# L1 attention: tiles of |q - k| moved from VectorE to ScalarE, and part of their sum moved into an adding DMA

## The chip, the cores and the metric

One core of one Trainium2 chip runs the whole program in one launch. The metric is the device time in microseconds (us). The kernel before takes 2713.21 us, the median of three runs (2711.84 to 2714.14).

## The reference, cut to what matters

The program is a small vision tower on 128 images of 64 tokens of 64 numbers: a wavelet tokeniser, attention, a mixture of experts, then the layer in question, and a routed MLP. The layer in question is an attention whose logits are L1 distances:

```python
v = (x @ wqv_w.T + wqv_b)            # 8 heads: q, vf, vb, 64 wide each
k = x[:, :, None, :] * wk[None, None]
a[b, s, t, h] = -sum_w |q[b, s, h, w] - k[b, t, h, w]| / 8     # w: 64 numbers
a = softmax over s of (a with one row of zeros added)
o = (a with vf + a^T with vb), summed over the heads
y = o * sigmoid(1.702 * o);  h = x + x_normed + y @ fanin_w.T + fanin_b
```

For one image the scores are 64 x 64 x 8 = 32768 sums over 64 numbers each; there are 128 images, 64 pairs of two.

## The kernel before, in words

Each engine has its own program, written by hand; semaphores (the dictionary `X`) order them. The layer runs over 64 pairs `q`, and over the two images `b` of a pair. `s = 2q + b` counts images.

**TensorE** writes, for one image, 16 tiles of q - k. A tile is 128 partitions x 1024 float32 (16 sums of 64 numbers in each partition), two banks of PSUM, written by two matmuls of 512 columns against `pick`, a matrix of 1 and -1, with the fp16 halves of q and k in `blocks` as the moving operand. `ORDER = "DADDADDADDADDADD"` says who takes each tile: D is VectorE (11 tiles, banks 0 to 3, two tiles in turn), A is ScalarE (5 tiles, banks 4 and 5 together). Between tiles, at fixed positions `k` of this order, TensorE does the rest of the layer (`extra`): values, queries and keys of pair q + 1 in float32 (`values_b`, `values_f`, `queries`, `low`, `keys`), the output of pair q - 2 (`turn_attn`, `attend`), and of pair q - 3 (`turn_y`, `fan_in`). Most of it lies in image 0.

**VectorE** reduces each D tile with absolute value to 16 scores (`reduce`), and has three small operations for each pair (`reciprocals`, `finish`, `gated`).

**ScalarE** writes the absolute values of each A tile to SBUF (`absolute`, into `absd0` or `absd1` by image), and moves the other results out of PSUM; its order is written out in `pair`. The exponentials of pair q - 1 stand near the end of image 1.

**GpSimd** waits for all five A tiles of an image and sums over w in a tree of halvings (`batch`): widths 32, 16, 8, 4, 2, and a last addition that writes the scores. `normalise` multiplies exponentials by reciprocals once a pair. ScalarE may write an image's first A tile once the batch of two images before is done (`X["pooled"]`).

**SyncE** issues the DMAs: `fill_blocks(p, b)` copies q and k into `blocks` (8 DMAs of 64 KB), `spread(p, b)` moves the scores of an image into the layout of the softmax (8 DMAs of 16 KB), `load_pair` fetches x. `fill_blocks` waits until all D tiles of the same image of the pair before are written, since it overwrites their operand (the last tile of the order is a D). In a pair SyncE issues: fill for image 1 of this pair, spread of image 0 and then image 1 of the pair before, fill for image 0 of the next pair, load.

`c_cols` is a constant that the tokeniser alone uses.

Of the kernel before, what the change touches and what calls it, by code (L numbers as in the profile page):

```python
# [19 lines left out]
P = 128  # L20
IMGS = 128
S = 64
D = 64
# [11 lines left out]

ORDER = "DADDADDADDADDADD"
ND, NA = ORDER.count("D"), ORDER.count("A")
W_SCALE = 64.0
LO_SCALE = 2048.0
# [70 lines left out]
def build(nc, a, out, scratch):  # L110

    with ExitStack() as ctx:
        def sb(name, shape, dt=F32):
            return ctx.enter_context(nc.sbuf_tensor(name, shape, dt))

        def sem(name):
# [12 lines left out]
        c_rows = sb("c_rows_sb", [P, 64])  # L129
        c_cols = sb("c_cols_sb", [7, 2, 8, P])  # L130
        tok_w = sb("tok_w", [7, D])
# [13 lines left out]

        absd0 = sb("absd0", [P, NA * 1024])
        kT = absd0[:, 2048:3072].rearrange("p (b a m) -> p b a m", b=2, a=4)
        qT = absd0[:, 3072:3584]
# [96 lines left out]

        absd = [t[:].rearrange("p (n w) -> p n w", w=D) for t in (absd0, absd1)]
        wk_b = big[0:D, 0:QK].rearrange("p (h d) -> p h d", d=D)
# [18 lines left out]
            "xs", "wk_in", "consts", "xT_ps", "xT_sb", "xTq", "q_ps", "k_ps", "qlo_ps", "klo_ps", "half", "tb0", "tb1",  # L266
            "diffD", "diffA", "red", "abs", "tree", "pooled", "spread0", "spread1", "exp", "zr", "attk", "attq_ps", "attq",
            "o_ps", "tanh", "y", "yT_ps", "yT", "fan_ps", "hx", "sum", "vb_ps", "vb", "vf_ps", "vf")}
# [53 lines left out]
        def _(sp):  # L322
# [53 lines left out]

            def fill_blocks(p, b, first):

                if not first:
                    sp.wait_ge(X["diffD"], ND * (2 * (p - 1) + b + 1))  # L380
                for kind in range(2):
                    for part in range(2):
                        if b == 0:
                            sp.wait_ge(X["half"], 4 * p + 2 * kind + part + 1)
                        for half in range(2):
                            src = qk[64 * b + 32 * half:64 * b + 32 * half + 32, kind, part, :]
                            to = slice(64 * kind + 32 * part, 64 * kind + 32 * part + 32)
                            dst = blocks[to, b, :, half, :] if kind == 0 else blocks[to, b, half, :, :]
                            sp.dma_start(dst, src.unsqueeze(1).to_broadcast([32, 2, QK])).then_inc(X[f"tb{b}"], 16)
# [15 lines left out]
            def pair(q, odd, at, following):  # L405
                fill_blocks(q, 1, at == 0)
                if at >= 1:
                    spread(q - 1, 1 - odd, 0, at == 1)
                    spread(q - 1, 1 - odd, 1, at == 1)
                fill_blocks(q + 1, 0, False)  # L410
                load_pair(following)
# [25 lines left out]
        def _(pe):  # L437
# [299 lines left out]
            def image(q, b, at, extra):  # L737

                s = 2 * q + b
                d = u = 0  # L740
                pe.wait_ge(X[f"tb{b}"], 16 * 8 * (q + 1))
                for k, path in enumerate(ORDER):
                    if path == "D":
                        if not (at == 0 and b == 0 and d < 2):
                            pe.wait_ge(X["red"], ND * s + d - 1)
                        unit, bank, done = 2 * d, 2 * ((b + d) % 2), "diffD"
                        d += 1
                    else:
                        if not (at == 0 and b == 0 and u == 0):
                            pe.wait_ge(X["abs"], NA * s + u)  # L750
                        unit, bank, done = 2 * (ND + u), 4, "diffA"
                        u += 1
                    for n in range(2):
                        mm = pe.matmul(ps[bank + n], pick[:, unit % 8 + n, :], blocks[:, b, unit // 16, unit // 8 % 2, :],  # L754
                                       start=True, stop=True)
                    mm.then_inc(X[done], 1)
                    extra(b, k)

            def pair(q, odd, at):
                def extra(b, k):  # L760
                    if b == 0:
                        if k == 0 and at >= 1:
                            values_b(q - 1, 1 - odd, at)
                        if k == 1 and at >= 3:
                            turn_y(q - 3)
                        if k == 3 and at >= 1:
                            values_f(q - 1, 1 - odd)
                        if k == 4 and at >= 3:
                            fan_in(q - 3)
                        if k == 8:  # L770
                            turn(q + 1, at)
# [80 lines left out]
        def _(act):  # L852
            act.dma_start(c_cols[:].rearrange("p a b c -> p (a b c)"), a["c_cols"]).then_inc(tok_in, 16)
            act.dma_start(tok_w[:], a["L0_tok_W"]).then_inc(tok_in, 16)
# [137 lines left out]
            def absolute(s, odd, u, first):  # L992

                act.wait_ge(X["diffA"], NA * s + u + 1)
                if u == 0 and not first:
                    act.wait_ge(X["pooled"], s - 1)
                nc.scalar.activation(absd[odd][:, 16 * u:16 * u + 16, :], pp[:, 4:6, :].rearrange("p n (h w) -> p (n h) w", w=D),  # L997
                                     ACT.Abs).then_inc(X["abs"], 1)

# [27 lines left out]
            def pair(q, odd, at):  # L1027
# [11 lines left out]
                absolute(s, 0, 3, first)  # L1039
                high_q(q + 1, False)  # L1040
                low(q + 1, 0)
                absolute(s, 0, 4, first)
                s += 1
# [13 lines left out]
                if at >= 1:  # L1057
                    exponentials(q - 1, 1, at == 1)

            act.wait_ge(pads, PADS)  # L1060
# [39 lines left out]
        def _(dve):  # L1100
# [253 lines left out]
            def reduce(s, odd, b, d):  # L1354
                dve.wait_ge(X["diffD"], ND * s + d + 1)
                bank = 2 * ((b + d) % 2)
                dve.tensor_reduce(score[:, odd, b, 16 * d:16 * d + 16],  # L1357
# [3 lines left out]
            def pair(q, odd, slot, at):  # L1361
                for b in range(2):
# [3 lines left out]
                    for d in range(ND):  # L1366
# [3 lines left out]
                        if b == 0 and d == 3 and at >= 3:  # L1370
                            finish(q - 3, slot)
                        if b == 1 and d == 8 and at >= 2:
                            gated(q - 2)
# [47 lines left out]
        def _(pool):  # L1421
# [36 lines left out]

            def batch(s, p, odd, b, at):

                x = absd[b]
                pool.wait_ge(X["abs"], NA * (s + 1))
                for m, w in enumerate((32, 16, 8, 4, 2)):
                    if m:
                        pool.wait_ge(X["tree"], 5 * s + m)
                    nc.gpsimd.tensor_tensor(x[:, :, 0:w], x[:, :, 0:w], x[:, :, w:2 * w], ALU.add).then_inc(X["tree"], 1)  # L1466
                pool.wait_ge(X["tree"], 5 * s + 5)
# [12 lines left out]
            def pair(q, odd, at):  # L1480
                if at >= 1:
                    batch(2 * q - 1, q - 1, 1 - odd, 1, at - 1)
                if at >= 2:
                    normalise(q - 2, at == 2)
                batch(2 * q, q, odd, 0, at)

            for q in range(4):
                pair(q, q % 2, q)
# [3 lines left out]
            last = PAIRS - 1  # L1492
            batch(2 * last + 1, last, 1, 1, 4)
            normalise(last - 1, False)
# [41 lines left out]
```

## Time and profile before

| | |
|---|---|
| median of 3 runs | 2713.21 us |
| the profiled execution's own time | 2712.7 us |
| its span | 2710.9 us |
| L1 attention, first to last tile of q - k | 720 to 2525 us of the span |
| busy over the whole span | TensorE 84%, VectorE 83%, GpSimd 65%, ScalarE 53% |
| TensorE granted clock in the layer | 1.00 |

A busy share over the whole span mixes stages; the layer's steady part, 1500 to 2000 us, is what to read. Busy times there are sums over 500 us; one pair takes 28.26 us, so 500 us hold 17.7 pairs. Durations of neighbouring instructions on one engine overlap a little, so that busy time can be less than count times duration.

### The profile page before, as it was taken

How to read it: one execution, taken by the hardware profiler on the slowest of the kernel's cores; microseconds unless marked ns; L12 is line 12 of the kernel's file. 1: busy time of each engine (PE TensorE's matmuls, PEld its weight loads, DVE VectorE, ACT ScalarE, POOL GpSimd, SP SyncE). 2: the span in 40 equal slices, each digit the busy share in tenths (PEclk: the TensorE clock that was granted, in tenths of full speed). 3: DMA queues.
4: the chain of work that ended last, by engine and by line, in shares of the span. 5: the costliest groups of instructions: out<-in, count | busy, mean ns of one | idle time of the engine just before them, and what ended most of it. 6: DMA issues, size and time to landing. Idle time of an engine off the chain costs nothing.

```text
span 2710.9 us, 44000 instructions
## 1 busy us (share of the span) xinstructions
PE 2267.9 (84%) x12251; PEld 958.0 (35%) x12251; DVE 2256.8 (83%) x2718; ACT 1435.1 (53%) x3127; POOL 1750.7 (65%) x1015
## 2 busy tenths in 40 slices
PE   5659999998488888888888888888888888888466
PEld 3433333333133333333333333333333333333245
DVE  2877787787799999999999999999999999999542
ACT  0325555554255556555565555655556555565234
POOL 0112233332388888888888888888888888888311
PEclk8879999999699999999999999999999999999678
DMA  5200000000121211211112111121111211112000
GB/s 129 58 1 1 1 0 0 0 0 0 27 50 49 50 43 48 49 48 49 43 48 49 48 48 44 48 49 48 48 44 48 49 48 48 44 48 49 14 12 19
DMA packets 163209, 101.97 MB, mean 38 GB/s; under 512 B 55773, under 2 KB 161182, under 8 KB 163039
## 3 DMA queue, kind: packets, MB, share of 16 engines
q1 hardware_dynamic: 162858, 101.41, 15.2%
q8 instruction: 18, 0.29, 0.0%
q10 hardware_dynamic: 316, 0.12, 0.0%
q14 instruction: 17, 0.14, 0.0%
HBM read 10.63 MB, written 4.19 MB: 5 GB/s over the span
## 4 chain that ended last, share of the span: by engine, by line
PE 64%; DVE 18%; issue 11%; ACT 3%; DVEq 2%; DMA 1%; POOL 1%; ACTq 0%; SPq 0%; POOLq 0%
PE pp L754 23%; DVE score L1357 12%; PE pp L594 5%; PE pp L725 3%; PE pp L696 3%; PE pp L615 2%; PE pp L681 2%; PE pp L673 2%; PE pp L619 2%; PE pp L669 2%; PE pp L679 2%; PE pp L620 2%; PE pp L616 2%; PE pp L689 2%; PE pp L586 2%
## 5 line engine op out<-in xcount | busy, mean ns | idle before, releaser
L1357 DVE TENSOR_REDUCE score<-pp 128x16 f32<-128x1024 f32 x1408 | 1651.1, 1218 | 158.4 <-PE pp L754 139.1
L1466 POOL TENSOR_TENSOR absd<-absd 128x2560 f32<-128x2560 f32 (+4 forms) x640 | 1450.1, 2266 | 262.1 <-ACT absd L997 221.9
L754 PE MATMUL pp<-blocks,pick 128*128 128x512 f16 x4096 | 1132.1, 382 | 178.9 <-DVE score L1357 139.8
L997 ACT ACTIVATE absd<-pp 128x1024 f32<-128x1024 f32 x640 | 655.1, 1024 | 535.9 <-PE pp L754 535.9
L754 PEld LDWEIGHTS pp<-blocks,pick 128*128 128x128 f16 x4096 | 311.5, 98 | 881.2 <-DVE score L1357 455.3
L1442 POOL TENSOR_TENSOR absd<-absd,yw 128x512 f32<-128x512 f32 x112 | 142.1, 1269 | 318.9 <-DVE yw L1279 318.9
L932 ACT ACTIVATE absd<-pp 128x512 f32<-128x512 f32 x256 | 150.8, 596 | 148.0 <-PE pp L616 146.5
L1295 DVE SCALAR_TENSOR_TENSOR absd<-pp,absd 128x512 f32<-128x512 f32 x256 | 172.4, 687 | 53.0 <-ACT absd L932 38.3
L980 ACT CAST qk<-pp 128x512 f16<-128x512 f32 x130 | 76.0, 585 | 191.2 <-PE pp L682 191.2
L1009 ACT ACTIVATE expd<-attn 128x65 f32<-128x65 f32 x512 | 155.9, 316 | 0.0
L594 PE MATMUL pp<-absd 128*64 128x512 f32 x512 | 138.1, 618 | 0.0
L696 PE MATMUL pp<-wqv,xT 96*64 96x256 f32 x512 | 69.4, 392 | 44.3 <-ACT vb L986 44.3
L1009 ACT ACTIVATION_READ_ACCUMULATOR expd<-attn 128x1 f32 x512 | 101.0, 197 | 0.0
L615 PE MATMUL pp<-x,absd 128*128 128x512 f16 x256 | 98.4, 384 | 0.5
L619 PE MATMUL pp<-x,absd 128*128 128x512 f16 x256 | 97.8, 382 | 0.2
L620 PE MATMUL pp<-x,absd 128*128 128x512 f16 x256 | 97.5, 381 | 0.0
L616 PE MATMUL pp<-x,absd 128*128 128x512 f16 x256 | 97.5, 381 | 0.0
L1279 DVE TENSOR_TENSOR yw<-pp,absd 128x512 f32<-128x512 f32 x112 | 77.1, 688 | 17.8 <-PE pp L594 15.3
L1503 POOL COPY xs<-xn 128x256 f32 x16 | 8.0, 528 | 127.7 <-PEq L849 93.0
L725 PEld LDWEIGHTS pp<-vb,attk 64*64 64x64 f32 x2048 | 71.0, 137 | 52.9 <-issue 52.6
L936 ACT COPY absd<-pp 128x512 f32<-128x512 f32 x128 | 74.9, 585 | 27.8 <-PE pp L586 18.9
L725 PE MATMUL pp<-vb,attk 64*64 64x64 f32 x2048 | 88.4, 227 | 0.0
(207 smaller groups left out, 2415.0 us busy)
## 6 DMA issues: line engine op xcount, KB each, us to landing
blocks<-qk SPq DMA_DIRECT2D x1032, 64.0 KB, 2.0
attn<-score SPq DMA_DIRECT2D x1024, 16.0 KB, 1.8
xs<-xn SPq DMA_DIRECT2D x66, 32.0 KB, 1.8
big<-in_wrb_t SPq DMA_DIRECT2D x1, 2064.0 KB
big<-in_x_rows SPq DMA_DIRECT2D x4, 512.0 KB, 6.1
token_rows<-big SPq DMA_DIRECT2D x8, 256.0 KB, 2.0
big<-in_L_ffn_w SPq DMA_DIRECT2D x4, 512.0 KB, 10.6
out<-big SPq DMA_DIRECT2D x16, 128.0 KB, 2.0
```

What stands on the lines that cost most here:

```text
L594: mm = pe.matmul(ps[4 + k % 2][64 * e:64 * e + 64, :], w3[:, 2 * k + e, :], hid[:, 2 * (k % 2) + e, :], start=True, stop=True)
L615: pe.matmul(ps[e], w12_hi[:, 0, 2 * k + e, :], x2[:, b, :], start=True, stop=False)
L616: pe.matmul(ps[e], w12_lo[:, 0, 2 * k + e, :], x2[:, b, :], start=False, stop=True).then_inc(C["h1_ps"], 1)
L619: pe.matmul(ps[2 + e], w12_hi[:, 1, 2 * k + e, :], x2[:, b, :], start=True, stop=False)
L620: pe.matmul(ps[2 + e], w12_lo[:, 1, 2 * k + e, :], x2[:, b, :], start=False, stop=True).then_inc(C["h2_ps"], 1)
L725: mm = pe.matmul(ps[7][at, P:P + D], attk[at, n, :], vb[at, odd, n, :], start=False, stop=(n == HEADS - 1))
L754: mm = pe.matmul(ps[bank + n], pick[:, unit % 8 + n, :], blocks[:, b, unit // 16, unit // 8 % 2, :], start=True, stop=True)
L997: nc.scalar.activation(absd[odd][:, 16 * u:16 * u + 16, :], pp[:, 4:6, :].rearrange("p n (h w) -> p (n h) w", w=D), ACT.Abs).then_inc(X["a ...
L1009: op = nc.scalar.activation(expd[:, n, :], attn[:, :, n], ACT.Exp, scale=-(float(D) ** -0.5), accum_out=zst[:, 0, n:n + 1])
L1295: dve.scalar_tensor_tensor(out=hid[:, 2 * (k % 2) + e, :], in0=ps[2 + e], scalar=1.0 / W_SCALE, in1=silu[:, e, :], op0=ALU.mult, op1=ALU.m ...
L1357: dve.tensor_reduce(score[:, odd, b, 16 * d:16 * d + 16], pp[:, bank:bank + 2, :].rearrange("p n (h w) -> p (n h) w", w=D), AX.X, ALU.add, ...
L1466: nc.gpsimd.tensor_tensor(x[:, :, 0:w], x[:, :, 0:w], x[:, :, w:2 * w], ALU.add).then_inc(X["tree"], 1)
```

## The change

- ORDER becomes `"DADDADDADDADADAD"`: 10 tiles to VectorE, 6 to ScalarE. Their D tiles alternate between the same bank pairs.
- An A tile is handled as two halves: each matmul writes one bank (4 or 5), signals by itself, and ScalarE takes the absolute values of one bank at a time (512 columns). TensorE fills one bank while the other is being read.
- `absd` is laid out as two planes `c` of half the width (w = 0..31, w = 32..63).
- For the first NT = 4 A tiles of an image the first halving, plane 1 onto plane 0, is made by a DMA that adds (`accum_op=ALU.add`), issued from GpSimd: 128 partitions x 2048 float32, 1 MB. GpSimd makes it for the two remaining tiles only. GpSimd issues it for the next image (`halve`) in the middle of the batch of this one, after the tree's levels 1 and 2, and waits there until the next image's fourth A tile is written.
- SyncE sends the scores of image 1 of the pair before between the two halves (queries, keys) of the next pair's fill; before, both spreads went ahead of that fill.
- TensorE does `values_f` at position 5 in place of 3. VectorE does `gated` after tile 7 in place of 8. ScalarE has its sixth `absolute` ahead of `high_k` in image 0, and after the exponentials in image 1.
- `c_cols` lies inside `absd0` and has no storage of its own.

```diff
-ORDER = "DADDADDADDADDADD"
+ORDER = "DADDADDADDADADAD"
+NT = 4
+        c_cols = absd0[0:7, 0:2048].rearrange("p (o c m) -> p o c m", o=2, c=8)
-        absd = [t[:].rearrange("p (n w) -> p n w", w=D) for t in (absd0, absd1)]
+        absd = [t[:].rearrange("p (c n w) -> p c n w", c=2, w=D // 2) for t in (absd0, absd1)]
 # SyncE: fill_blocks takes kinds=range(2) as a parameter
             def pair(q, odd, at, following):
                 fill_blocks(q, 1, at == 0)
                 if at >= 1:
                     spread(q - 1, 1 - odd, 0, at == 1)
+                fill_blocks(q + 1, 0, False, (0,))
+                if at >= 1:
                     spread(q - 1, 1 - odd, 1, at == 1)
-                fill_blocks(q + 1, 0, False)
+                fill_blocks(q + 1, 0, True, (1,))
                 load_pair(following)
 # TensorE
-                        unit, bank, done = 2 * d, 2 * ((b + d) % 2), "diffD"
+                        unit, bank, done = 2 * d, 2 * (d % 2), "diffD"
-                        if not (at == 0 and b == 0 and u == 0):
-                            pe.wait_ge(X["abs"], NA * s + u)
-                        unit, bank, done = 2 * (ND + u), 4, "diffA"
+                        for n in range(2):
+                            if not (at == 0 and b == 0 and u == 0):
+                                pe.wait_ge(X["abs"], 2 * NA * s + 2 * u + n - 1)
+                            unit = 2 * (ND + u) + n
+                            pe.matmul(ps[4 + n], pick[:, unit % 8, :], blocks[:, b, unit // 16, unit // 8 % 2, :],
+                                      start=True, stop=True).then_inc(X["diffA"], 1)
-                        if k == 3 and at >= 1:
+                        if k == 5 and at >= 1:
                             values_f(q - 1, 1 - odd)
 # ScalarE
-                act.wait_ge(X["diffA"], NA * s + u + 1)
-                if u == 0 and not first:
-                    act.wait_ge(X["pooled"], s - 1)
-                nc.scalar.activation(absd[odd][:, 16 * u:16 * u + 16, :], pp[:, 4:6, :].rearrange("p n (h w) -> p (n h) w", w=D),
-                                     ACT.Abs).then_inc(X["abs"], 1)
+                for n in range(2):
+                    act.wait_ge(X["diffA"], 2 * NA * s + 2 * u + n + 1)
+                    if u == 0 and n == 0 and not first:
+                        act.wait_ge(X["pooled"], s - 1)
+                    nc.scalar.activation(absd[odd][:, :, 16 * u + 8 * n:16 * u + 8 * n + 8, :].rearrange("p c n w -> p n c w"),
+                                         ps[4 + n].rearrange("p (h c w) -> p h c w", c=2, w=D // 2), ACT.Abs).then_inc(X["abs"], 1)
                 high_q(q + 1, False)
+                absolute(s, 0, 4, first)
                 low(q + 1, 0)
-                absolute(s, 0, 4, first)
+                absolute(s, 0, 5, first)
...
                     exponentials(q - 1, 1, at == 1)
+                absolute(s, 1, 5, first)
 # VectorE: bank = 2 * (d % 2); gated at d == 7
 # GpSimd
+            def halve(s, p, b):
+                pool.wait_ge(X["abs"], 2 * NA * s + 2 * NT)
+                pool.sem_inc(X["taken"], 1)
+                pool.dma_start(absd[b][:, 0, 0:16 * NT, :].rearrange("p n w -> p (n w)"),
+                               absd[b][:, 1, 0:16 * NT, :].rearrange("p n w -> p (n w)"),
+                               accum_op=ALU.add).then_inc(X[f"half{b}"], 16)
+
+            def level(s, x, m, w):
+                pool.wait_ge(X["tree"], 5 * s + m)
+                nc.gpsimd.tensor_tensor(x[:, :, 0:w], x[:, :, 0:w], x[:, :, w:2 * w], ALU.add).then_inc(X["tree"], 1)
+
+            def batch(s, p, odd, b, at, following):
+                x = absd[b][:, 0]
+                rest = slice(16 * NT, 16 * NA)
+                pool.wait_ge(X["abs"], 2 * NA * (s + 1))
+                nc.gpsimd.tensor_tensor(x[:, rest, :], x[:, rest, :], absd[b][:, 1, rest, :], ALU.add).then_inc(X["tree"], 1)
+                pool.wait_ge(X[f"half{b}"], 16 * (p + 1))
+                level(s, x, 1, 16)
+                level(s, x, 2, 8)
+                if following:
+                    halve(s + 1, p + b, 1 - b)
+                level(s, x, 3, 4)
+                level(s, x, 4, 2)
```

## Rows read from the trace of the kernel before

**Rows 1.** The page: span and instructions; the chain that ended last, shares by engine.

```profile
span 2710.9 us, 44000 instructions
PE 64%; DVE 18%; issue 11%; ACT 3%; DVEq 2%; DMA 1%; POOL 1%; ACTq 0%; SPq 0%; POOLq 0%
```

**Rows 2.** Busy time by stretch: us, PE, PEld, DVE, ACT, POOL, PEclk, DMA share, GB/s.

```profile
1500.00:2000.00 500.00, 439.10 (x2491) 174.55 (x2489) 460.26 (x444) 296.30 (x678) 430.71 (x233) 1.00 0.19 48
```

**Rows 3.** Groups by form, 1500:2000: line, engine, operation, shapes, count | busy, mean ns | idle before.

```profile
L1357 DVE TENSOR_REDUCE score<-pp 128x16 f32<-128x1024 f32 x390 | 457.6, 1218 | 39.7 <-PE pp L754 34.5
L1466 POOL TENSOR_TENSOR absd<-absd 128x2560 f32<-128x2560 f32 x35 | 195.2, 5577 | 52.9 <-ACT absd L997 52.9
L997 ACT ACTIVATE absd<-pp 128x1024 f32<-128x1024 f32 x177 | 181.2, 1024 | 149.0 <-PE pp L754 149.0
L1466 POOL TENSOR_TENSOR absd<-absd 128x1280 f32<-128x1280 f32 x36 | 104.7, 2908 | 2.8
L1466 POOL TENSOR_TENSOR absd<-absd 128x640 f32<-128x640 f32 x36 | 55.0, 1527 | 2.8
L1009 ACT ACTIVATE expd<-attn 128x65 f32<-128x65 f32 x144 | 43.8, 316 | 0.0
L1466 POOL TENSOR_TENSOR absd<-absd 128x320 f32<-128x320 f32 x36 | 31.0, 861 | 2.8
L1477 POOL TENSOR_TENSOR attk<-expd,zst 128x512 f32<-128x512 f32 x18 | 18.8, 1042 | 0.0
L1470 POOL TENSOR_TENSOR score<-absd 128x80 f32<-128x80 f32 x36 | 11.5, 321 | 5.2 <-POOL absd L1466 4.5
L986 ACT COPY vb<-pp 128x512 f32<-128x512 f32 x18 | 10.4, 580 | 0.0
```

**Rows 4.** Waits, 1500:2000: who <- for whom: us in total, times, longest.

```profile
POOL absd L1466 <- ACT absd L997: 52.9, 35, 1.8
DVE score L1357 <- PE pp L754: 34.5, 89, 1.0
PE pp L696 <- ACT vb L986: 12.5, 18, 0.7
PE pp L754 <- ACT absd L997: 7.6, 35, 0.3
```

**Rows 5.** Timeline of SyncE's queue, one pair: start, us, line, what, count.

```profile
1507.64 5.08 SPq L389 DMA_DIRECT2D blocks<-qk  x8
1513.03 11.57 SPq L398 DMA_DIRECT2D attn<-score  x16
1524.82 5.30 SPq L389 DMA_DIRECT2D blocks<-qk  x8
1535.90 5.09 SPq L389 DMA_DIRECT2D blocks<-qk  x8
```

**Rows 6.** Timeline of GpSimd in the same pair.

```profile
1507.48 11.61 POOL L1466 TENSOR_TENSOR absd<-absd 128x2560 f32<-128x2560 f32 x5 [1.25 <-ACT absd L997]
1519.26 0.32 POOL L1470 TENSOR_TENSOR score<-absd 128x80 f32<-128x80 f32 x1 [0.17 <-POOL absd L1466]
1522.34 11.67 POOL L1466 TENSOR_TENSOR absd<-absd 128x2560 f32<-128x2560 f32 x5 [1.76 <-ACT absd L997]
```

**Rows 7.** DMA issues, 1500:2000 (KB, us to landing); moved GB/s, 50:135 in 40 slices.

```profile
blocks<-qk SPq DMA_DIRECT2D x283, 64.0 KB, 2.0
attn<-score SPq DMA_DIRECT2D x281, 16.0 KB, 1.8
...
GB/s 253 217 217 208 172 199 199 216 206 173 84 305 64 0 0 0 0 0 0 155 420 420 101 4 0 0 0 0 0 0 0 0 0 0 8 0 0 0 0 0
```

**Rows 8.** The chain that ended last, in order of time: start, us, what.

```profile
1511.84 1.08 PE pp L696 x8
...
1517.68 0.86 PE pp L669 x2
...
1520.71 0.86 PE pp L754 x4
```

More of the change, by code:

```diff
@@ L129, in build @@
         c_rows = sb("c_rows_sb", [P, 64])
-        c_cols = sb("c_cols_sb", [7, 2, 8, P])
         tok_w = sb("tok_w", [7, D])
@@ L266, in build @@
             "xs", "wk_in", "consts", "xT_ps", "xT_sb", "xTq", "q_ps", "k_ps", "qlo_ps", "klo_ps", "half", "tb0", "tb1",
-            "diffD", "diffA", "red", "abs", "tree", "pooled", "spread0", "spread1", "exp", "zr", "attk", "attq_ps", "attq",
+            "diffD", "diffA", "red", "abs", "taken", "half0", "half1", "tree", "pooled", "spread0", "spread1", "exp", "zr", "attk", "attq_ps", "attq",
             "o_ps", "tanh", "y", "yT_ps", "yT", "fan_ps", "hx", "sum", "vb_ps", "vb", "vf_ps", "vf")}
@@ L375, in _, with fill_blocks @@
             sp.dma_start(wk_b, a["L1_attn_wk"].partition_broadcast(D)).then_inc(X["wk_in"], 16)
-            def fill_blocks(p, b, first):
+            def fill_blocks(p, b, first, kinds=range(2)):
                 if not first:
                     sp.wait_ge(X["diffD"], ND * (2 * (p - 1) + b + 1))
-                for kind in range(2):
+                for kind in kinds:
                     for part in range(2):
@@ L745, in image @@
                             pe.wait_ge(X["red"], ND * s + d - 1)
-                        unit, bank, done = 2 * d, 2 * ((b + d) % 2), "diffD"
+                        unit, bank, done = 2 * d, 2 * (d % 2), "diffD"
                         d += 1
                     else:
-                        if not (at == 0 and b == 0 and u == 0):
-                            pe.wait_ge(X["abs"], NA * s + u)
-                        unit, bank, done = 2 * (ND + u), 4, "diffA"
+                        for n in range(2):
[4 more added lines that the diff above has]
+                                      start=True, stop=True).then_inc(X["diffA"], 1)
                         u += 1
+                        extra(b, k)
+                        continue
                     for n in range(2):
@@ L765, in extra @@
                             turn_y(q - 3)
-                        if k == 3 and at >= 1:
-                            values_f(q - 1, 1 - odd)
                         if k == 4 and at >= 3:
                             fan_in(q - 3)
+                        if k == 5 and at >= 1:
+                            values_f(q - 1, 1 - odd)
                         if k == 8:
@@ L852, in _ @@
         def _(act):
-            act.dma_start(c_cols[:].rearrange("p a b c -> p (a b c)"), a["c_cols"]).then_inc(tok_in, 16)
+            act.dma_start(c_cols.rearrange("p a b c -> p (a b c)"), a["c_cols"]).then_inc(tok_in, 16)
             act.dma_start(tok_w[:], a["L0_tok_W"]).then_inc(tok_in, 16)
@@ L1355, in reduce @@
                 dve.wait_ge(X["diffD"], ND * s + d + 1)
-                bank = 2 * ((b + d) % 2)
+                bank = 2 * (d % 2)
                 dve.tensor_reduce(score[:, odd, b, 16 * d:16 * d + 16],
@@ L1371, in pair @@
                             finish(q - 3, slot)
-                        if b == 1 and d == 8 and at >= 2:
+                        if b == 1 and d == 7 and at >= 2:
                             gated(q - 2)
@@ L1457, in _ @@
             nc.gpsimd.tensor_tensor(h[:], h[:], xn[:, 0:PAIRS, :], ALU.add).then_inc(X["hx"], 1)
[L1459 to L1466, printed above, removed]
+            def halve(s, p, b):
[19 more added lines that the diff above has]
+                level(s, x, 4, 2)
                 pool.wait_ge(X["tree"], 5 * s + 5)
@@ L1481, in pair @@
                 if at >= 1:
-                    batch(2 * q - 1, q - 1, 1 - odd, 1, at - 1)
+                    batch(2 * q - 1, q - 1, 1 - odd, 1, at - 1, True)
                 if at >= 2:
                     normalise(q - 2, at == 2)
-                batch(2 * q, q, odd, 0, at)
+                batch(2 * q, q, odd, 0, at, True)
+            halve(0, 0, 0)
             for q in range(4):
@@ L1492, in _ @@
             last = PAIRS - 1
-            batch(2 * last + 1, last, 1, 1, 4)
+            batch(2 * last + 1, last, 1, 1, 4, False)
             normalise(last - 1, False)
```

## The prediction

> **What bounds the kernel now.** I read the page first. It has TensorE at 64% of the chain that ended last and VectorE at 18% [rows 1], but that chain runs through every stage, and the change touches only the L1 attention. So next the steady stretch 1500:2000 [rows 2]. SyncE's fill for image 1 begins at 1507.64 and again at 1535.90 [rows 5]: a pair takes 28.26 us, an image 14.13, and 500 us hold 17.7 pairs. Per pair that is VectorE 460.26/17.7 = 26.0 us busy, TensorE 24.8, GpSimd 24.3, ScalarE 16.7; the clock is 1.00, so nothing is to be had from it. VectorE is the bound: it idles 2.25 us a pair, of which 34.5/17.7 = 1.95 is waiting for TensorE's tiles [rows 4]. GpSimd isn't the bound: it waits for ScalarE's last A tile, 52.9 us in 35 images, 1.5 us each [rows 3, 4]. But its batch takes 12.1 us from first addition to scores (1507.48 to 1519.58) of an image of 14.13 [rows 6]. VectorE can't simply hand a tile to ScalarE: a sixth of a tree more would be 14.3 us of GpSimd, which is why part of the tree goes to a DMA here.
>
> **VectorE.** A reduction costs 457.6/390 = 1.173 us of busy time [rows 3]. Two fewer per pair: 26.0 - 2.35 = 23.65 us. With all of the old idle kept (2.25) the pair takes 25.9. `gated` one tile earlier costs nothing: `attend` ends at position 9, and ScalarE's tanh follows the A tile of position 10, before VectorE is done with its tile 7.
>
> **TensorE.** It makes the same 64 matmuls for tiles. Four take 0.86 us back to back, and a float32 product of 512 columns 0.86 too [rows 8]. Image 0 holds 32 x 0.215 = 6.9 for tiles, four products (values_b, queries, low, keys) 3.4, low's second matmul 0.2, values_f 1.1: 11.6 us. To that come waits for ScalarE, per pair 12.5/17.7 = 0.7 before values_f and 7.6/17.7 = 0.4 before A tiles [rows 4], and small transposes: 12.7 to 13. VectorE wants only 10 x 1.173 + 0.4 = 12.1 there. So in image 0 TensorE sets the pace, and the second removed tile is only partly paid out. Moving values_f from position 3 to 5 gives ScalarE two tiles more to copy vb; I count up to 0.5 us for it and let it stand against the tile-by-tile waits that are new.
>
> **ScalarE.** A copy of 512 columns takes 0.58, an absolute of 1024 took 1.024 [rows 3]. Before: 10 x 1.02 = 10.2 us a pair; after: 24 halves, 13.9. Its load goes from 16.7 to 20.4 of some 26 us, so in sum it isn't the bound; its order can be. In image 1 the A tiles stand at positions 10, 12 and 14 and four exponentials (0.3 each) between the first two. From position 10 on: 1.16 (tile) + 1.2 (exponentials) + 0.58 (half of the next) + hand-overs 0.2 = 3.1 us until bank 4 is free for position 14, 3.7 for bank 5; then the last D tile, 0.43 and its latency, is there at 4.3. VectorE's three tiles in that stretch last 3.5. So image 1 costs 11.7 + 0.2 + 0.8 = 12.7 to 12.9. Both images: 25.6 to 25.9, the same as the first way.
>
> **GpSimd.** A pass costs 2.09 ns for each element beyond 1280: (5577 - 2908)/1280 [rows 3]. The new batch: 1024 elements 2.37, 1536 elements 3.44, 768 1.80, 384 0.99, 192 about 0.55, the last 96 0.34: 9.5 us, with gaps 9.9, against 12.1. Issuing the adding DMA costs GpSimd something that no row shows. From below 0.64, SyncE's issue of a fill (5.08/8) [rows 5]; from above 2.9, GpSimd's pass over 1280 elements [rows 3]. I take 1.0, near the issue. With half of a `normalise` (0.5) an image has 11.4 us of work for 13: room, if the transfer is on time.
>
> **The adding transfer.** Its time X, from issue to landing, is the unknown on which the forecast hangs. It reads two planes and writes one: 1.05 MB written, 2.1 MB read. From below: 1.05 MB at the 420 GB/s of the best slices plus the 2.0 us of a fill's landing, 4.5 us. From above: 2.1 MB at the 217 GB/s of the slower slices, plus 2.0, plus 1.0 to issue: 12.7 us [rows 7]. The runs here are 8 KB in each partition, so I take the faster slices and the double reading: 5.0 + 2.0, and 0.5 for the engines being 19% busy with other transfers [rows 2]: 7.5 us. Now the ring. GpSimd issues the transfer of image s + 1 after level 2 of image s, and level 1 of image s + 1 needs it landed; levels 1 and 2 are 3.44 + 1.80 + 0.15 = 5.4. An image can't be shorter than X + 5.4. With 7.5 that is 12.9: just under the 13 of the engines. It reaches the time of before (14.13) at X = 8.7.
>
> The Trainium skill speaks to this ("DMA: Bandwidth & Descriptors", the table of measured sizes): a plain load of 1 MB issued from GpSimd keeps the DMA engines busy 6.15 us. With the page's fixed 2.0 us the plain transfer would be 8.2 us, an image 13.6 and the program some 2646 us. No run here shows it yet.
>
> **The other ring through GpSimd.** ScalarE's first A tile waits for the batch of two images before. That batch holds the wait for the next image's fourth A tile (position 10 of 16: 9.0 us into the image of 13.1, absolutes by 10.2), then issue 1.0 and levels 3, 4 and the last 2.2: over at 13.4. ScalarE wants its tile 13.9 after the start. It holds with 0.5 us.
>
> **SyncE.** The same 33 DMAs. The queries' fill now waits in front of the spread of image 1: it waits for the D tiles of image 0 (at half the pair), and behind it are 4 + 8 + 4 issues. Before, half of the spread was already gone by then; 1524.82 to 1530.12 had the fill alone. From half pair to `blocks` ready: 15 x 0.645 + 2.0 + 0.1 = 11.8 us, of 13.1 at hand [rows 5, 7]. The spread lands at 13.1 + 0.1 + 11 x 0.645 + 1.8 = 22.1 of the pair; the exponentials want it at 22.8. Both hold, with 1.3 and 0.7 us, where before they had several.
>
> The transfer for image 1 is issued 23 us into the pair and runs until 29, exactly beside the last fill. The Trainium skill says (same page, on queues and rings) that an engine takes turns between its queues, a whole packet at a time; a 1 KB run of the fill would then wait for an 8 KB run each time. It speaks against this change, and gives 1 to 2 us on a landing that has 1.3 to spare.
>
> Collisions of this kind are likely on any account, the engines being 19% busy before and perhaps 60% after ((5.0 x 2)/26 more). I add 0.4 us a pair to 25.9.
>
> **Sum.** 26.3 us a pair against 28.26: 1.95 x 64 = 125 us. The start is the same; the last batch is 2 us shorter but waits once for its transfer, so I put the tail at nothing (within 2 us). 2712.7 - 125 = 2588 us. The profiled execution is 0.5 us under the median of the runs, which doesn't matter here. `c_cols`, the banks' order and the half-width planes of `absd` cost nothing: ScalarE's output stays runs of 32 numbers, which I bound at 0 to 0.1 us a half (24 halves, 2.4 us of an engine with 5.6 to spare).
>
> **Rivals.**
> - *The transfer's time sets the pace (slower).* X above 8.7: the reading side slower than copies, or the descriptors of 128 partitions slow to write. At X = 10 an image takes 15.4, a pair 30.8: 2712.7 + 64 x 2.54 = 2875 us; at 9.2, 29.2: 2773. For it: both bounds leave room, and GpSimd stands idle in the ring. Against it: 7.5 needs no slow path. 0.17.
> - *The transfer binds, but mildly.* X from 7.8 to 8.7, for instance 8.2: pair 27.2, 2645 us. 0.14.
> - *SyncE's queue sets the pace.* After the half pair there are 16 issues and a landing, and a landing beside the transfer can be later by as much as the transfer's 5 us. From 2.3 us late (14.1 for half a pair) it loses all the gain; at 2.6, a pair of 28.8, 2748 us. 0.07.
> - *The relief is swallowed* by ScalarE's longer order or by TensorE in image 0, with the pair at 28.2 again. Against it: 1.95 of the waits are TensorE's being late by a little, not a chain as long as the pair. 2712 us. 0.04.
> - *Nothing collides,* and values_f pays: pair 25.2, 2517 us. 0.08.
>
> Forecast: 0.50, its own range 2560 to 2625. Range for 8 in 10: 2515 to 2755, from the good end of nothing colliding to SyncE's queue and the first part of the slow transfer. Faster by over 0.2% (5 us, what a measurement can tell here): 0.50 + 0.14 + 0.08 = 0.72; within: 0.04; slower: 0.17 + 0.07 = 0.24.
>
> **What would show it.** VectorE's reductions 20 a pair, busy some 23.7 us of 26.3; its idle time mostly on TensorE's tiles in image 0 and at the end of image 1. ScalarE's halves 0.58 us. GpSimd's passes 2.4, 3.4, 1.8, 1.0, 0.55. Between `halve` and level 1 the landing: under 7.7 us right, over 8.7 the first rival, and then GpSimd would show a wait for a DMA before its second pass and ScalarE a wait for the batch. If the fill were late, TensorE's first tile of image 0 would wait for a DMA. The forecast is wrong if VectorE's idle time a pair is above 3.5 us, or if the pair is limited by any wait for a transfer.

## The result, and the profile after

The changed kernel takes 2843.02 us (median of 4 runs, 2840.11 to 2848.64) against 2712.53 us before: 1.048 times as long, 95% interval 1.047 to 1.050. The forecast of 2588 us has the wrong sign.

First the page of the changed kernel: the span, busy time, two DMA queues, the chain by engine and by line, and the DMA issues with their time to landing.

```profile
span 2846.8 us, 46562 instructions
...
PE 2343.8 (82%) x12251; PEld 1014.3 (36%) x12251; DVE 2119.3 (74%) x2590; ACT 1618.6 (57%) x4023; POOL 1581.6 (56%) x1143
...
q0 software_dynamic: 18432, 134.23, 23.7%
q1 hardware_dynamic: 162858, 101.41, 14.6%
...
PE 46%; DVE 16%; SPq 15%; DMA 10%; issue 6%; ACT 4%; DVEq 2%; POOL 0%; ACTq 0%; POOLq 0%
DVE score L1372 11%; SPq L401 10%; PE pp L766 8%; DMA blocks<-qk 7%; PE pp L760 5%; SPq L392 5%; PE pp L600 4%; PE pp L687 2%; PE pp L621 2%; PE pp L679 2%; PE pp L625 2%; PE pp L695 2%; PE pp L675 2%; PE pp L622 2%; PE pp L626 2%
...
absd<-absd POOLq DMA_DIRECT2D x128, 1024.0 KB, 7.5
blocks<-qk SPq DMA_DIRECT2D x1032, 64.0 KB, 2.3
```

VectorE and GpSimd have less to do than before, ScalarE more, as planned, and no engine but TensorE is busy for over 74% of the span. New in the chain are SyncE's queue (SPq) with 15% and DMA with 10%; before, they had 0 and 1% [rows 1]. In the steady stretch 1500:2000 the busy times [rows 2] and the waits [rows 4] have become (who <- for whom: us in total, times, longest):

```profile
1500.00:2000.00 500.00, 427.32 (x2313) 177.46 (x2313) 390.45 (x377) 320.18 (x858) 354.59 (x246) 0.94 0.52 112
```

```profile
DVE score L1372 <- PE pp L766: 107.3, 102, 5.7
POOL absd L1478 <- ACT absd L1010: 70.0, 26, 7.7
POOL absd L1484 <- DMA absd<-absd: 49.7, 33, 2.2
PE pp L766 <- DMA blocks<-qk: 36.1, 9, 5.9
```

The line to read is the last, though it is the smallest: TensorE waits for a fill (the copy of q and k into `blocks`) 9 times in some 17 pairs, 3.2 to 5.9 us each. Before, no tile waited for one in this stretch. The granted clock fell from 1.00 to 0.94. The timeline tells which pairs they are. SyncE's queue (L392 fills, L401 spreads) over two pairs:

```profile
1508.90 6.87 SPq L392 DMA_DIRECT2D blocks<-qk  x8
1516.07 4.99 SPq L401 DMA_DIRECT2D attn<-score  x8
1528.03 3.31 SPq L392 DMA_DIRECT2D blocks<-qk  x4
1531.46 4.99 SPq L401 DMA_DIRECT2D attn<-score  x8
1536.56 2.63 SPq L392 DMA_DIRECT2D blocks<-qk  x4
1539.34 0.55 SPq L406 DMA_DIRECT2D xs<-xn  x1
1541.40 6.94 SPq L392 DMA_DIRECT2D blocks<-qk  x8
1548.46 5.09 SPq L401 DMA_DIRECT2D attn<-score  x8
1554.97 3.90 SPq L392 DMA_DIRECT2D blocks<-qk  x4
1558.98 5.00 SPq L401 DMA_DIRECT2D attn<-score  x8
1564.09 2.63 SPq L392 DMA_DIRECT2D blocks<-qk  x4
1566.86 0.55 SPq L406 DMA_DIRECT2D xs<-xn  x1
1568.48 6.89 SPq L392 DMA_DIRECT2D blocks<-qk  x8
```

Pairs begin at 1508.90, 1541.40 and 1568.48: 32.5 us, then 27.08. The first seven pairs of the layer are nearly all long; after them long and short mostly take turns. Of 63 such distances in the layer 33 are over 31 us, 33.4 on average. GpSimd's issues of the transfer for image 1 in the same pairs, and what the chain of waits has at the end of the second:

```profile
1538.79 0.87 POOL L1478 DMA_DIRECT2D absd<-absd  x1 [1.96 <-ACT absd L1010]
...
1565.74 0.87 POOL L1478 DMA_DIRECT2D absd<-absd  x1 [1.06 <-ACT absd L1010]
```

```profile
1565.48 0.59 SPq L392
1566.11 5.62 DMA blocks<-qk
1571.73 0.14 issue
1571.87 1.03 PE pp L766 x2
```

At the end of the first pair the last fill is issued at about 1538.6 (the fourth of 1536.56 to 1539.19), 0.2 us before the transfer; the next pair's tiles don't wait. At the end of the second it is issued at 1566.11, 0.4 us behind the transfer, and lands 5.6 us later in place of 2.0 [rows 7]. The issues had been slower too: from the first one after the half pair (1554.97) to the last took 11.1 us. A long pair begins.

How late the fill lands hangs on how far the transfer is ahead. In the nine long pairs of the stretch it took 5.4 to 5.6 us to land when the transfer had been issued 0.3 to 0.4 us before it, 6.4 at 0.5, and 8.1 at 0.55 (twice), as here:

```profile
1625.75 0.87 POOL L1478 DMA_DIRECT2D absd<-absd  x1 [0.92 <-ACT absd L1010]
...
1626.29 8.12 DMA blocks<-qk
```

The start of the long pair at 1508.90, by stretches (columns as in rows 2):

```profile
1509.00:1512.20 3.20, 0.00 (x0) 0.00 (x0) 1.13 (x1) 1.16 (x4) 2.10 (x2) 0.60 1.10 223
1512.20:1516.00 3.80, 3.74 (x8) 1.64 (x9) 1.33 (x2) 0.46 (x1) 1.91 (x2) 0.50 0.73 158
1516.00:1518.00 2.00, 1.79 (x9) 0.79 (x7) 1.20 (x2) 1.82 (x6) 1.92 (x2) 0.88 0.23 57
```

TensorE has nothing for 3.2 us while the DMA engines are full, and then works at a granted clock of 0.50, that is 1.2 GHz, until about 1516; values_b lasts 1.92 us where it lasted 1.02. This long pair costs 5.4 us more than the short one: 3.4 of waiting, and for the rest the low clock accounts nearly (3.8 us of work at half the clock, so 1.9 us more; an estimate).

### The profile page after: what moved, and what is told of

Read it like the earlier page. It is cut to its first block, busy times and chain, and to the rows that moved or that the text cites. A ratio compares the mean times of both kernels' runs of the same rounds, so it can differ in the third digit from the quotient of the medians.

```text
span 2846.8 us, 46562 instructions
## 1 busy us (share of the span) xinstructions
PE 2343.8 (82%) x12251; PEld 1014.3 (36%) x12251; DVE 2119.3 (74%) x2590; ACT 1618.6 (57%) x4023; POOL 1581.6 (56%) x1143
## 3 DMA queue, kind: packets, MB, share of 16 engines
q0 software_dynamic: 18432, 134.23, 23.7%
## 4 chain that ended last, share of the span: by engine, by line
PE 46%; DVE 16%; SPq 15%; DMA 10%; issue 6%; ACT 4%; DVEq 2%; POOL 0%; ACTq 0%; POOLq 0%
DVE score L1372 11%; SPq L401 10%; PE pp L766 8%; DMA blocks<-qk 7%; PE pp L760 5%; SPq L392 5%; PE pp L600 4%; PE pp L687 2%; PE pp L621 2%; PE pp L679 2%; PE pp L625 2%; PE pp L695 2%; PE pp L675 2%; PE pp L622 2%; PE pp L626 2%
## 5 line engine op out<-in xcount | busy, mean ns | idle before, releaser
L1372 DVE TENSOR_REDUCE score<-pp 128x16 f32<-128x1024 f32 x1280 | 1510.0, 1220 | 434.0 <-PE pp L766 425.5
L1010 ACT ACTIVATE absd<-pp 128x512 f32<-128x512 f32 x1536 | 834.1, 596 | 496.6 <-PE pp L760 485.7
L1484 POOL TENSOR_TENSOR absd<-absd 128x1536 f32<-128x1536 f32 (+3 forms) x512 | 903.0, 1764 | 211.7 <-DMA absd<-absd 191.4
L766 PE MATMUL pp<-blocks,pick 128*128 128x512 f16 x2560 | 780.4, 396 | 197.2 <-DMA blocks<-qk 137.4
L760 PE MATMUL pp<-blocks,pick 128*128 128x512 f16 x1536 | 512.8, 396 | 86.7 <-ACT absd L1010 71.9
L766 PEld LDWEIGHTS pp<-blocks,pick 128*128 128x128 f16 x2560 | 214.9, 100 | 564.4 <-issue 252.1
L1492 POOL TENSOR_TENSOR absd<-absd 128x1024 f32<-128x1024 f32 x128 | 300.3, 2346 | 70.4 <-ACT absd L1010 70.4
L760 PEld LDWEIGHTS pp<-blocks,pick 128*128 128x128 f16 x1536 | 149.0, 100 | 419.5 <-ACT absd L1010 248.6
L1478 POOL DMA_DIRECT2D absd<-absd x128 | 111.7, 873 | 288.3 <-ACT absd L1010 284.0
L944 ACT ACTIVATE absd<-pp 128x512 f32<-128x512 f32 x256 | 151.1, 597 | 147.9 <-PE pp L622 145.6
L695 PE MATMUL pp<-wqv,xT 96*128 96x512 f32 x128 | 94.9, 834 | 0.0
```

The lines of the kernel that those rows point to most:

```text
L760: pe.matmul(ps[4 + n], pick[:, unit % 8, :], blocks[:, b, unit // 16, unit // 8 % 2, :], start=True, stop=True).then_inc(X["diffA"], 1)
L1010: nc.scalar.activation(absd[odd][:, :, 16 * u + 8 * n:16 * u + 8 * n + 8, :].rearrange("p c n w -> p n c w"), ps[4 + n].rearrange("p (h c ...
L1372: dve.tensor_reduce(score[:, odd, b, 16 * d:16 * d + 16], pp[:, bank:bank + 2, :].rearrange("p n (h w) -> p (n h) w", w=D), AX.X, ALU.add, ...
L1492: nc.gpsimd.tensor_tensor(x[:, rest, :], x[:, rest, :], absd[b][:, 1, rest, :], ALU.add).then_inc(X["tree"], 1)
```

## The experiments

Theory F: the loss is the load of the adding transfer, behind which the last fill of the next pair's image 0 is queued. Rivals: R, the ring through GpSimd; E, the engines' own order. Every ratio is to the kernel before, run beside it (2711 to 2712 us).

**A tiny transfer.** All waits and issues stay, 64 KB move in place of 1 MB.

```diff
-                pool.dma_start(absd[b][:, 0, 0:16 * NT, :]..., absd[b][:, 1, 0:16 * NT, :]...,
+                pool.dma_start(absd[b][:, 0, 0:4, :]..., absd[b][:, 1, 0:4, :]...,
```

> The changed kernel, but the adding transfer moves 128 of its 2048 numbers in each partition (64 KB in place of 1 MB); the other scores of ScalarE's first four tiles lack half of their sum. All semaphores and the issue on GpSimd stay. Theory F: the loss is the load of the transfer, in whose queue the last fill of the next pair's first image stands (landing 5.6 us against 2.0), with TensorE's clock falling after the wait. Then no pair waits for the fill, all take about 27.0 us, what the undisturbed pairs take already: 2712 - 64 x 1.25 = 2632 us, and the clock is 1.00. Theory R, the ring through GpSimd (landing 7.5 + levels 1 and 2): 26.5 to 27, also some 2620. Theory E, the engines' own order (ScalarE in image 1, TensorE in image 0) is what costs: nothing changes much, 2800 to 2843.

Measured 2629.5 us, ratio 0.970 (0.969 to 0.972). Clock 1.00 in the stretch, no wait for a fill, pairs of 26.94 us. Theory E falls as the main cause. The load of the transfer costs 2843.0 - 2629.5 = 213 us, more than the whole gain of the rest. It doesn't tell F from R, since both the bytes and the transfer's landing (2.4 us in place of 7.5) went.

**SyncE's old order.**

```diff
                     spread(q - 1, 1 - odd, 0, at == 1)
-                fill_blocks(q + 1, 0, False, (0,))
-                if at >= 1:
                     spread(q - 1, 1 - odd, 1, at == 1)
-                fill_blocks(q + 1, 0, True, (1,))
+                fill_blocks(q + 1, 0, False)
```

> The changed kernel with SyncE's order of before: both spreads, then the whole fill for the next pair's first image. The spread of image 1 can then start when GpSimd's batch is over (13.2 us into an undisturbed pair by the trace) and doesn't wait behind the queries' fill; the last fill is issued some 1.0 to 1.5 us earlier, ahead of the adding transfer in every pair. Theory F in its sharp form (it is the order of arrival at the DMA queues that decides): no long pairs, 2630 to 2660 us. If the new order is harmless or helps: 2843 or slower, since the fill is then 8 issues later behind a batch that ends late.

Measured 2835.0 us, 1.047 (1.045 to 1.049). It is neither the gain expected nor a loss: long and short pairs take turns as before, with waits of 3.5 us, and the time is within 8 us of the changed kernel's. The spread of image 1 waits for GpSimd's batch, and the batch now holds the wait for the next image's A tile; behind it stand the same 16 issues, and the last fill again meets the transfer. "Scores sent between the next blocks" is neither the cause nor a cure.

**The transfer of image 1 behind the fill.**

```diff
                 pool.wait_ge(X["abs"], 2 * NA * s + 2 * NT)
+                if b == 1:
+                    pool.wait_ge(X["tb0"], 16 * 8 * (p + 2))
```

> The changed kernel, but GpSimd issues the adding transfer of image 1 only when the fill for the next pair's first image has landed. Theory F: the fills land in 2.0 us, the alternation of 27.1 and 32.9 us pairs goes; the transfer starts 1 to 2 us later, and GpSimd's ring (7.6 + 5.4) has room for about 1: pairs of 27.0 to 27.6, 2635 to 2680 us. Theory R: the ring was already tight, each us of delay is paid in full, 28.5 or more, 2730 us and up.

Measured 2832.7 us, 1.045 (1.043 to 1.047). The alternation went, the pairs take 30.1 us on average (29.6 to 30.7 in the steady stretch). The waits:

```profile
POOL absd L1486 <- DMA absd<-absd: 75.2, 34, 3.6
...
POOL absd L1480 <- DMA blocks<-qk: 55.3, 16, 3.7
...
ACT absd L1010 <- POOL score L1505: 28.4, 15, 2.1
```

GpSimd stands 3.5 us for the fill, then the transfer runs beside the fill of image 1, whose eight issues take 8.5 to 8.9 us where they took 5.1 [rows 5], and lands 3 us too late for its batch. ScalarE in turn waits for the batch. The time is what theory R expected. But the edit does more than move the transfer: GpSimd waits in the middle of its batch, so the rest of the batch, the scores and ScalarE's first tile behind them, is held up as well. A 1 MB transfer issued behind the whole batch, without this, was not run.

**No transfer at all.** NT = 0, GpSimd makes every level itself.

> The changed kernel without any adding transfer: GpSimd makes the first level for all six tiles itself (3072 numbers, 6.6 us by 2.09 ns each). The result is the full one. GpSimd then works 6.6 + 3.46 + 1.80 + 0.98 + 0.5 + 0.35 = 13.7 us an image with 0.5 of gaps, and 1.04 a pair for the normalising: 29.4 us a pair. All theories of the transfer: 2712 + 64 x 1.15 = 2786 us, GpSimd over 95% busy, no wait for a fill: faster than the changed kernel, slower than before. Theory E: 2843 or more.

Measured 2793.5 us, 1.030 (1.029 to 1.032), near the 2786 computed from GpSimd's passes; it is busy 484 of 500 us. The new split of tiles with the whole tree left on GpSimd loses, but less than with the transfer.

**The transfer in four pieces**, one tile each: runs of 2 KB in place of 8 KB.

```diff
-                pool.dma_start(absd[b][:, 0, 0:16 * NT, :]...
+                for t in range(NT):
+                    pool.dma_start(absd[b][:, 0, 16 * t:16 * t + 16, :]...
```

> The changed kernel with the adding transfer of 1 MB issued as four of 256 KB, one tile each: the same bytes in runs of 2 KB in place of 8 KB. The load on the DMA engines is the same. Theory P (a fill's runs of 1 KB take turns with the transfer's runs, so that it waits for one whole 8 KB run, 0.59 us, each time): with 2 KB runs the last fill lands in 2.5 to 3.5 us in place of 5.6 and fewer or no pairs wait for it. Against it stand three more issues of 0.87 us on GpSimd for each image, which has 1 to 2 us of waiting to give: 2700 to 2760 us. Theory L (the load as such, bytes over bandwidth): the fill still lands in 5 us or more, and with the longer issue it is 2843 or slower.

Measured 2822.5 us, 1.041 (1.039 to 1.042). TensorE's waits for a fill are 0.3 to 1.5 us in place of 3.2 to 5.9, and where the chain of waits shows the last fill (seven times) it lands in 3.4 to 3.7 us: near theory P, far from theory L's 5 or more. But the four pieces also start one after the other, so that fewer bytes are ahead of the fill. And GpSimd pays for four issues in place of one:

```profile
1525.89 3.54 POOL L1479 DMA_DIRECT2D absd<-absd  x4
```

It is busy 450 of 500 us, and by the trace the ring sets the pace. The time was 60 us above the expectation's upper end: the issues were counted, but not that level 1 could start only 9.3 us after the first of them (1535.20), against 7.5 for the transfer in one.

**Half the transfer.** NT = 2, GpSimd makes the first level of four tiles.

```diff
-NT = 4
+NT = 2
```

> NT = 2: the transfer carries two tiles (512 KB, runs of 4 KB), GpSimd makes the first level for four (2048 numbers, 4.5 us in place of 2.35). The transfer should take 2.0 + 2.35 + 0.9 = 5.2 us. GpSimd's own work is 4.5 + 3.46 + 1.8 + 0.98 + 0.5 + 0.35 + 0.87 and gaps, 12.9 an image, 26.8 a pair with the normalising. Theories P and L: the wait for the fill is at most 2 us, and the pair is GpSimd's and the engines' 27.0 to 27.6: 2635 to 2680 us, faster than before.

Measured 2636.2 us, 0.973 (0.971 to 0.974): faster than before. Landing, GpSimd in one pair (which begins at 1526.37), and SyncE's last fill of it:

```profile
absd<-absd POOLq DMA_DIRECT2D x37, 512.0 KB, 4.6
```

```profile
1527.70 4.53 POOL L1492 TENSOR_TENSOR absd<-absd 128x2048 f32<-128x2048 f32 x1 [0.31 <-ACT absd L1010]
...
1551.43 0.87 POOL L1478 DMA_DIRECT2D absd<-absd  x1
```

```profile
1547.81 2.62 SPq L392 DMA_DIRECT2D blocks<-qk  x4
```

The longer first level makes GpSimd late: its transfer for image 1 leaves at 25.1 us of the pair, 1.6 us after the last fill (1549.8). So it isn't clear from this run whether the bytes or the timing helped; the next two tell it for three tiles. Half the transfer issued just ahead of the last fill was not run.

**Three tiles.** NT = 3.

> NT = 3: 768 KB in runs of 6 KB, GpSimd's first level for three tiles 3.4 us. Between: transfer 6.4 us, GpSimd 11.8 an image, room of 1.5. Theories P and L: the last fill is delayed by up to 2.6 us in some pairs: 2680 to 2780 us. If it comes out at the changed kernel's 2843, the alternation doesn't depend on the size of the transfer but on its being there.

Measured 2896.4 us, 1.068 (1.066 to 1.070): outside the expected range, and slower than with the larger transfer. The pairs take 31.4 us on average (30.7 to 32.2), and each waits 2.4 to 2.5 us for its fill:

```profile
PE pp L766 <- DMA blocks<-qk: 39.6, 16, 2.5
```

The transfer of image 1 is issued at 1549.21, and the last fill's four issues stand at 1548.78 to 1552.32: three of them are behind it, and the last lands 5.8 us after its issue. The long start of the pair keeps the fill late, and the transfer, timed by GpSimd, keeps its place: the collision seems to hold itself (read from the timeline, not tested).

**Three tiles, the transfer issued after the batch.**

```diff
                 level(s, x, 2, 8)
-                if following:
-                    halve(s + 1, p + b, 1 - b)
...
                                         ALU.add).then_inc(X["pooled"], 1)
+                if following:
+                    halve(s + 1, p + b, 1 - b)
```

> NT = 3, with the next image's transfer issued after the whole batch (behind the scores) in place of after level 2, some 2.2 us later. In NT = 3 as it was, the transfer for image 1 left 26.0 us into a pair of 31.1 and the last fill was issued at 28.5, so every pair waited. Theory T (timing: it matters on which side of the transfer the last fill is issued): now the transfer leaves 27 us into the pair, after a last fill issued at 24, nothing waits for the fill; but the ring is longer, 6.2 + 3.4 + 1.8 + 2.2 = 13.8 us an image: 27.6 to 28.2 a pair, 2670 to 2720 us. Theory L (the load as such): still about 31 us a pair, 2880 us or more.

Measured 2755.6 us, 1.016 (1.014 to 1.018): 141 us less with the same bytes. No tile waits for a fill any more, pairs take 28.8 us on average, and the ring is what is left:

```profile
POOL absd L1484 <- DMA absd<-absd: 67.1, 35, 3.2
```

ScalarE waits for GpSimd's batch 32 times, 23.9 us in all. It is slower than expected by 35 us: issue to landing is 6.5 us and not 6.2, and the rest of the ring 7.8 and not 7.4. (The expectation's sum also comes to 13.6 and not to the 13.8 written there.)

**Half the transfer with SyncE's old order.**

> NT = 2 and SyncE's order of before. It tells what the new order is worth once the transfer is small. The spread of image 1 waits for GpSimd's batch, over at about 13.5 to 14 us of the pair with the longer first level, and behind it are 16 issues: 24.2 with the landing 26. If the new order is worth anything, this is slower than NT = 2 alone by the fill's wait, 0.3 to 1 us a pair: 20 to 60 us. If the order is worth nothing, as with the large transfer, within 10 us of it.

Measured 2633.0 us, 0.971 (0.970 to 0.973), within 4 us of the new order. The order is worth nothing here either.

**The load, on the kernel before.** GpSimd issues a 1 MB adding transfer on an idle buffer for each image. No addition waits for it; GpSimd only makes sure, before each issue, that the one before has landed.

```diff
+                    if m == 1:
+                        pool.wait_ge(X["dummy"], 16 * s)
+                        pool.sem_inc(X["taken"], 1)
+                        pool.dma_start(big[:, 0:2048], big[:, 2048:4096], accum_op=ALU.add).then_inc(X["dummy"], 16)
```

> The kernel before with one part of the change alone, the load: GpSimd issues, after the first level of each batch, an adding transfer of 1 MB between two parts of a buffer that the layer doesn't use, and nothing waits for it (it adds work that changes no result). In the kernel before the last fill is issued by 22.5 us of a pair of 28.3 and has 4 us to spare. The transfer of image 0's batch leaves at about 20.5, beside that fill, and delays its landing by 3 to 4 us: just covered. Theory T/P: 2712 to 2760 us, GpSimd's issues (0.87 each) within its waiting. Theory L, load hurts wherever it is: 2800 or more.

Measured 2803.1 us, 1.034 (1.032 to 1.036): at the expectation of the rival, 92 us more than without it. I had counted only a later landing. The issues beside the transfer get longer too, 7.05 us for eight in place of 5.30 [rows 5]. And not all of it is the load: with its own issue (0.87 us) and an idle 0.66 us ahead of it GpSimd's batch takes 13.5 us in place of 12.1 [rows 6], the spread of image 1 waits for the batch, and the last fill stands behind the spread. It is issued 18.7 us into the pair that begins at 1517.77, in place of 17.2 [rows 5]. Together these use up the 4 us that the fill had:

```profile
1536.46 7.05 SPq L389 DMA_DIRECT2D blocks<-qk  x8
```

```profile
PE pp L754 <- DMA blocks<-qk: 20.7, 12, 2.6
```

So a batch made longer and a large transfer beside the last fill cost the old kernel 92 us together. How much of it is the load alone wasn't measured.

**ScalarE's order in image 1**, on the kernel with the tiny transfer.

```diff
+                absolute(s, 1, 4, first)
                 if at >= 1:
                     exponentials(q - 1, 0, at == 1)
-                absolute(s, 1, 4, first)
+                absolute(s, 1, 5, first)
                 if at >= 1:
                     exponentials(q - 1, 1, at == 1)
-                absolute(s, 1, 5, first)
```

> The kernel with the tiny transfer (the first four A tiles' scores lack half of their sum), and ScalarE takes the fifth A tile of image 1 before the first four exponentials in place of after them. There TensorE waited 1.0 us for ScalarE's bank and VectorE 1.06 us for its last tile. If that is what keeps the undisturbed pair at 26.94 and not at the forecast's 26.3, it becomes 26.0 to 26.3: 2570 to 2590 us, against 2629.5. If the exponentials only move the wait to the sixth tile: 2615 to 2630.

Measured 2597.8 us, 0.958 (0.956 to 0.960), pairs of 26.44 us: between the two expectations. VectorE's wait for tiles, with the tiny transfer and then with the new order as well:

```profile
DVE score L1372 <- PE pp L766: 58.4, 94, 1.1
```

```profile
DVE score L1372 <- PE pp L766: 42.5, 95, 0.9
```

The exponentials ahead of the fifth tile cost 0.5 us a pair, 32 us in all.

**Both together**: NT = 2 and this order.

> NT = 2 together with ScalarE's fifth A tile of image 1 before the exponentials; the full result. In NT = 2 alone GpSimd had 0.5 us of waiting in a pair of 26.93, and the engines' order kept the same 26.94. The reordering frees the engines to 26.4 (the tiny transfer's 26.44); GpSimd then has no waiting left and holds the pair at 26.4. 2600 us, within 2592 to 2615. If the earlier transfer of image 1 meets the last fill (it left 25.1 us into the pair, the last fill was issued at 23.4), pairs of 30 come back: above 2650.

Measured 2614.5 us, 0.9645 (0.9628 to 0.9661), at the upper end of the expectation: 97 us faster than the kernel before. GpSimd is busy 485 of 500 us and, by that, the bound. Some fills are issued in 6.9 us; what the remaining 0.2 us a pair above the tiny transfer's time is made of, I didn't separate.

## Why the prediction was wrong, by its own steps

- *VectorE, TensorE, GpSimd's passes*: right. A reduction 1.22 us mean and two fewer; passes 2.35, 3.46 and 1.80 us against 2.37, 3.44 and 1.80.
- *ScalarE and both images, 25.9 us*: the mechanism was right (the last D tile of image 1 late behind the exponentials), the size not. Without collisions the sum has a pair of 25.9; with the tiny transfer it is 26.94. VectorE waits 58.4 us in 18.6 pairs for TensorE's tiles, 3.1 us each, where the sum kept 2.25 us of idle time in all. One of these waits, 1.06 us, is the one behind the exponentials (the term "0.8"); values_f's 0.5 us, which I "let stand against the tile-by-tile waits", wasn't measured by itself. This is 68 us of the error (2629.5 against the 2562 that 25.9 gives), of which the changed order gives back 32. The other half is open.
- *The transfer, X = 7.5*: right, 7.5 us from issue to landing, 0.87 to issue against 1.0. The agreement is partly luck: its parts (the rate, the double reading, 0.5 for other load) weren't measured one by one. The likeliest rival, a slow transfer, did not happen.
- *The step that failed is the last one ahead of the sum: "I add 0.4 us a pair"* for collisions. The prediction had the place (the transfer of image 1 beside the last fill) and the slack of 1.3 us, and had the landing late by 1 to 2 us. From half pair to `blocks` ready it had 15 x 0.645 + 2.0 = 11.7 us, and with the tiny transfer that is what it takes (9.8 + 2.0). Beside the large one the same issues took 11.1 and the landing 5.6: 16.7, late by 5.0 where 1.3 to 1.5 were to spare, and up to 2.5 more where the landing took 8.1. That leaves the 3.4 us of waiting, and the low clock after it added some 2 us. In place of 0.4 the load costs 213/64 = 3.3 us a pair, as an average of pairs with and without a collision: 2.9 us a pair too few, 187 us of the 255 by which the forecast missed.
- *Rivals*: SyncE's queue, given 0.07, is the one that came, and was priced too low (2748 us), since its own price of 5 us at the most was set aside for 2.6 and the clock was left out. "The clock is 1.00, so nothing is to be had from it" was true of the profile before, and no bound on what could be lost.
- *The rule on turns between queues* that spoke against the change (the Trainium skill, "DMA: Bandwidth & Descriptors", on queues and rings) is borne out by the traces as far as they go. The profile has 144 packets to a transfer (18432 for 128), so one for each of its 128 runs of 8 KB and 16 for the signals. (The Trainium skill's page lets a packet hold some 9 to 17 descriptors; that a turn is one run was the prediction's own reading.) They took 23.7% of 16 engines' 2846.8 us, 0.59 us each, and a fill brings four runs of 1 KB to each engine: 4 x 0.6 = 2.4 us by turns for one fill, more with a second fill in the same queue (an estimate). Measured in the long pairs were 3.4 to 3.6 us more in most and 6.1 at the most, a step of some 2.5. Pieces of 2 KB brought the wait from 3.2 or more to about 1. Against it stands the kernel with three tiles: shorter runs, of 6 KB, and a landing of 5.8 us. The Trainium skill's plain 1 MB (same page, the table of measured sizes, 6.15 us busy) put the transfer at 8.2 us; measured were 7.5.

What is shown: the load of the 1 MB transfer costs 213 us, against the same kernel with a tiny one; and at NT = 3, with the same bytes, issuing the transfer after the batch, behind the last fill, is worth 141 us. Read from the trace of the changed kernel: that the load acts through the last fill there (nine waits in nine long pairs, none in the short ones). No run settles it at NT = 4: the one that took the fill's waits away gained 10 us only, since the ring through GpSimd then cost as much. Argued only: that the turns of 8 KB runs make the landing late. A fill that stands behind all bytes issued before it would explain the latest landings as well: where it took 8.1 us it landed 0.2 us after the transfer, and at NT = 3 about 1 us after it (by the transfer's median time). Why the alternation becomes a steady state at NT = 3 is read from timelines, not tested.

## What to carry to other kernels

Work given to the DMA engines isn't free though they are idle 80% of the time: what counts is which small transfer with a deadline is issued just behind it, and how much that one may be late. For each transfer on the path write down its slack, and add to it the whole running time of any large one beside it, not a share (here up to 6.1 us of the 7.5). And where TensorE comes to wait for that, price the low clock after the wait too.

## What the runs showed of the hardware that was not expected

- Adding transfers between two parts of SBUF, issued from GpSimd, took from issue to landing 2.4 us for 64 KB, 4.6 for 512, 6.2 for 768 and 7.5 for 1024, nearly a line of 2.1 us and 5.4 us for each MB, and 0.87 us of GpSimd each whatever their size.
- SyncE's issues of a fill get slower beside a large transfer (0.63 us each to 0.86, and 1.07 in the gated kernel), though they belong to another queue.
- Each of TensorE's waits for a fill in the stretch 1500:2000, 3.2 to 5.9 us in the changed kernel and 2.4 to 2.5 with three tiles, was followed by a time at 1.2 GHz, of some 4 us where the granted clock was read closely. With the extra load on the old kernel waits of 2.0 to 2.2 us were followed by it in some pairs and in others not.
- A smaller transfer was slower (768 KB, 2896 us, against 1 MB, 2843 us) because of when it left.
